# Decoder kernel: where the context of batches 1 to 3 is loaded and split into halves

## What is computed

```python
x = _layernorm(x + _L0_attn_ref(x, ...))             # causal self attention, 32 heads of 16, rope
x = _layernorm(x + _L0_xattn_ref(x, ctx_4096, ...))  # cross attention, 32 heads of 128, 8 key/value heads, 1601 keys
x = _layernorm(x + _L0_ffn_ref(x, ...))              # base matrix plus top 2 of 28 LoRA experts of rank 8
```

## Time and profile before

| | |
|---|---|
| median of 3 runs | 2960.67 us (2955.37 to 2963.62) |
| profiled execution, its own time | 2956.6 us |
| its span, first to last instruction | 2954.8 us |
| mean granted clock of PE | 0.979 of full speed |
| busy: PE, DVE, ACT, POOL | 93%, 71%, 67%, 56% of the span |

### The profile page before, as it was taken

One profiled execution on the slowest core, in us unless ns is written; L12 is line 12 of the kernel. 1 busy time (PEld: TensorE's weight loads), 2 busy tenths in 40 slices (PEclk: granted clock), 3 DMA queues, 4 the chain that ended last, 5 costly groups with the idle time before them and its releaser, 6 DMA issues.

```text
span 2954.8 us, 60508 instructions
## 1 busy us (share of the span) xinstructions
PE 2760.3 (93%) x20272; PEld 2576.1 (87%) x20272; DVE 2100.3 (71%) x4364; ACT 1973.2 (67%) x4392; POOL 1660.6 (56%) x1663
## 2 busy tenths in 40 slices
PE   7899999998899999999899999999988999999996
PEld 6789999998679999999768999999967899999995
DVE  5477777778557878787755877777766587878785
ACT  4476676767457777677655877777756576767673
POOL 4288897947115656565611656555552265656564
PEclk9999999999899999999999999999989999999998
DMA  5446464612311212121331112121232121212112
GB/s 186 139 165 216 160 231 158 211 58 101 119 48 44 94 51 94 51 94 51 122 102 44 63 67 76 69 74 71 78 119 86 42 74 57 89 55 90 55 55 100
DMA packets 97921, 285.10 MB, mean 96 GB/s; under 512 B 9936, under 2 KB 18256, under 8 KB 94416
## 3 DMA queue, kind: packets, MB, share of 16 engines
q1 hardware_dynamic: 97616, 281.24, 27.3%
HBM read 237.16 MB, written 44.04 MB: 95 GB/s over the span
## 4 chain that ended last, share of the span: by engine, by line
PE 67%; issue 11%; POOL 9%; ACT 5%; DVE 5%; DMA 2%; DVEq 0%; ACTq 0%; SPq 0%; POOLq 0%
PE bank L1030 39%; PE dn L1030 14%; PE sp L1030 9%; POOL kept_s L527 4%; ACT ph L714 2%; PE sp L1161 1%; POOL orw L546 1%; PE sp L1169 1%; POOL ol L550 1%; ACT pn L641 1%; PE sp L1101 1%; PE sp L1248 1%; DVE mcol L909 1%; POOL hib L517 1%; ACT sp L719 1%
## 5 line engine op out<-in xcount | busy, mean ns | idle before, releaser
L527 POOL TENSOR_TENSOR kept_s<-kept_s,mrow 128x512 f32<-128x512 f32 (+1 forms) x896 | 1062.3, 1215 | 596.8 <-ACT mrow L704 596.7
L920 DVE TENSOR_TENSOR pl<-sp,ph 128x512 fp32r<-128x512 f32 (+1 forms) x896 | 576.9, 644 | 79.3 <-ACT sp L719 75.8
L714 ACT ACTIVATE ph<-kept_s 128x512 fp32r<-128x512 f32 (+1 forms) x896 | 534.1, 596 | 45.7 <-POOL kept_s L527 42.8
L719 ACT ACTIVATE sp<-kept_s 128x512 f32<-128x512 f32 (+1 forms) x896 | 506.1, 565 | 2.1 <-DVE sua L928 2.1
L1030 PE MATMUL dn<-ph,vh 128*128 128x256 f32 (+1 forms) x1664 | 489.4, 294 | 2.2 <-DVE pl L920 1.7
L1030 PE MATMUL dn<-ph,vl 128*128 128x256 f32 (+1 forms) x1664 | 471.4, 283 | 0.0
L1030 PE MATMUL dn<-pl,vh 128*128 128x256 f32 (+1 forms) x1664 | 470.7, 283 | 0.0
L928 DVE TENSOR_TENSOR sua<-sp,sua 128x512 f32<-128x512 f32 (+1 forms) x640 | 400.2, 625 | 0.0
L696 ACT ACTIVATE kept_s<-bank 128x512 f32<-128x512 f32 x384 | 228.5, 595 | 232.0 <-PE bank L1030 231.4
L696 ACT ACTIVATE kept_s<-sp 128x512 f32<-128x512 f32 x384 | 228.6, 595 | 193.0 <-PE sp L1030 192.6
L1030 PEld LDWEIGHTS dn<-ph,vh 128*128 128x128 f32 (+1 forms) x1664 | 316.5, 190 | 10.3 <-DVE pl L920 3.4
(11 more groups left out here) (149 smaller groups left out, 6967.4 us busy)
## 6 DMA issues: line engine op xcount, KB each, us to landing
wqx<-wq SPq DMA_DIRECT2D x128, 512.0 KB, 3.3
wox<-wo SPq DMA_DIRECT2D x64, 1024.0 KB, 4.8
wk<-wk SPq DMA_DIRECT2D x32, 512.0 KB, 3.3
wvx<-wv SPq DMA_DIRECT2D x16, 1024.0 KB, 5.6
raw<-in_ctx_t SPq DMA_DIRECT2D x48, 200.0 KB, 2.4
wqk<-in_ws SPq DMA_DIRECT2D x17, 513.0 KB, 4.0
raw<-in_wq_in SPq DMA_DIRECT2D x32, 256.0 KB, 3.8
wq<-hib SPq DMA_DIRECT2D x32, 256.0 KB, 2.0
```

Of the source, the lines that this page charges most:

```text
L527: nc.gpsimd.tensor_tensor(kept_s[:, n % 2, i:z, :], kept_s[:, n % 2, i:z, :], mrow[:, n % 2, :].unsqueeze(1).broadcast_to([P, z - i, S]), ...
L714: nc.scalar.activation(ph[:, k % PH, 0:cols], src, ACT.Exp, scale=XSCALE).then_inc(ph_ok, 1)
L719: nc.scalar.activation(pbank[k % 2][:, 0:cols], src, ACT.Exp, scale=XSCALE).then_inc(pr_ok, 1)
L920: nc.vector.tensor_tensor(pl[:, k % PH, 0:cols], src, ph[:, k % PH, 0:cols], ALU.subtract).then_inc(pl_ok, 1)
```

## The change

For batch 0 nothing changes in the self attention. The 16 pieces of batch b+1 (b = 0, 1, 2) are now made in the cross attention of batch b: SP issues the load of piece i at slot 184 + 2i, and ACT's copy and POOL's subtraction of piece i stand at slot 186 + 2i, the last ones at slot 216, each at the end of its engine's slot. A slot g holds POOL's shift of slot g + 4, so the pieces fall behind the shifts s = 1, 3, 5 of head 27, s = 0, 2, 4, 6 of head 28, s = 1, 3, 5 of head 29, s = 0, 2, 4, 6 of head 30 and s = 1, 3 of head 31. ACT's copy waits besides for the last K job, since it overwrites the context. The order of the pieces is now by columns first. The self attention of batches 1 to 3 holds no piece any more.

```diff
--- before.py
+++ after.py
@@ -153,17 +153,30 @@
 HEAD_W = 3
 
 
-def raw_at(b, m, i):
-
-    if b == 0:
-        return m * len(SA_RAW) + i
-    return NM * len(CTX_PIECES) * b + W_N + m * len(CTX_PIECES) + i
+def raw_at(m, i):
+
+    return m * len(SA_RAW) + i
+
+
+CTX_ORDER = [(m, k) for k in range(len(CTX_PIECES)) for m in range(DC)]
+CTX_LOAD, CTX_HIGH = NSL * 26 + 2, NSL * 26 + 4
+
+
+def ctx_piece(g, start):
+
+    i, odd = divmod(g - start, 2)
+    return [i] if not odd and 0 <= i < CTX_N else []
+
+
+def ctx_at(b, i):
+
+    return CTX_N * b + W_N + i
 
 
 def raw_of_weight(k):
 
     if k < NM * SA_W:
-        return raw_at(0, k // SA_W, 2 * (k % SA_W) + 1)
+        return raw_at(k // SA_W, 2 * (k % SA_W) + 1)
     return NM * len(SA_RAW) + k - NM * SA_W
 
 
@@ -414,13 +427,12 @@
                         sp.dma_start(wqk[:, :], ws[m + 1, :, 0:W_QK]).then_inc(wqk_ld, 16)
                         sp.wait_ge(s_vp, at(t, 1, 1))
                         sp.dma_start(wv[:, :], ws[m + 1, :, W_QK:W_QK + D]).then_inc(wv_ld, 16)
-                    for k in range(len(CTX_PIECES)):
-                        load_context(b, m, k, raw_at(b, m, 2 * k if b == 0 else k))
-                        if b == 0:
-                            if k:
-                                store_weight(m * SA_W + k - 1)
-                            if k < SA_W:
-                                load_weight(m * SA_W + k)
+                    for k in range(len(CTX_PIECES) if b == 0 else 0):
+                        load_context(0, m, k, raw_at(m, 2 * k))
+                        if k:
+                            store_weight(m * SA_W + k - 1)
+                        if k < SA_W:
+                            load_weight(m * SA_W + k)
                 if b == 0:
                     load_k(0, 0)
                     load_q(0)
@@ -463,6 +475,9 @@
                             load_k(b * NP + (c + 1) // 2, (c + 1) % 2)
                         elif c + 1 == XKV:
                             load_k(b * NP + NP, 0)
+                    for i in ctx_piece(g, CTX_LOAD):
+                        if b + 1 < nb:
+                            load_context(b + 1, *CTX_ORDER[i], ctx_at(b + 1, i))
                     for j in JOBS[g]:
                         used(j)
                 sp.wait_ge(sc_mm, (b + 1) * NHB * NSL)
@@ -501,10 +516,10 @@
             pool.sem_inc(ot_ok, 1)
             nc.gpsimd.memset(vx[:, :, :, :], 0.0).then_inc(s_vz, 1)
 
-            def ctx_low_part(b, m, k, r):
+            def ctx_low_part(n, m, k, r):
 
                 a, z = CTX_PIECES[k]
-                pool.wait_ge(split_hi, b * CTX_N + m * len(CTX_PIECES) + k + 1)
+                pool.wait_ge(split_hi, n + 1)
                 nc.gpsimd.tensor_tensor(ctxl[:, m, a:z], raw[:, r % 2, 0:z - a], ctxh[:, m, a:z],
                                         ALU.subtract).then_inc(raw_free, 1)
 
@@ -553,10 +568,10 @@
                 pool.wait_ge(x_ld, at(b, 32, 32))
                 for tb in range(TB):
                     nc.gpsimd.tensor_tensor(xres[:, tb, :], xres[:, tb, :], bos[:, :], ALU.add).then_inc(bias_ok, 1)
-                for m in range(NM):
+                for m in range(NM if b == 0 else 0):
                     for k in range(len(CTX_PIECES)):
-                        ctx_low_part(b, m, k, raw_at(b, m, 2 * k if b == 0 else k))
-                        if b == 0 and k < SA_W:
+                        ctx_low_part(m * len(CTX_PIECES) + k, m, k, raw_at(m, 2 * k))
+                        if k < SA_W:
                             split_weight(m * SA_W + k)
                 pool.wait_ge(xt_ps, at(b, 2 * TB, TB))
                 for tb in range(TB):
@@ -568,6 +583,9 @@
                         shift_scores(b, h, s)
                     for h in head_of(g, HEAD_END):
                         finish_head(b, h)
+                    for i in ctx_piece(g, CTX_HIGH):
+                        if b + 1 < nb:
+                            ctx_low_part(CTX_N * (b + 1) + i, *CTX_ORDER[i], ctx_at(b + 1, i))
                     h, s = divmod(g, NSL)
                     if b == 0 and 0 <= h < NHB and s in PIECE_SLOTS:
                         k = NM * SA_W + HEAD_W * h + PIECE_SLOTS.index(s)
@@ -593,8 +611,10 @@
                     nc.scalar.activation(dst[:, :, tb * P:(tb + 1) * P],
                                          mx[:, tb, :].rearrange("p (c n) -> p c n", c=DC), ACT.Copy).then_inc(xt_ok, 1)
 
-            def high_part(hi, src):
-                nc.scalar.activation(hi, src, ACT.Copy).then_inc(split_hi, 1)
+            def ctx_high_part(m, k, r):
+                a, z = CTX_PIECES[k]
+                act.wait_ge(raw_ld[r % 2], 16 * (r // 2 + 1))
+                nc.scalar.activation(ctxh[:, m, a:z], raw[:, r % 2, 0:z - a], ACT.Copy).then_inc(split_hi, 1)
 
             for b in range(nb):
                 act.wait_ge(s_vz, b + 1)
@@ -651,13 +671,8 @@
                         take_qk(m + 1)
                     if i == 7 and m + 1 < NM:
                         take_v(m + 1)
-                    if i in (1, 3, 5, 7) and m < NM:
-
-                        k = i // 2
-                        r = raw_at(b, m, 2 * k if b == 0 else k)
-                        a, z = CTX_PIECES[k]
-                        act.wait_ge(raw_ld[r % 2], 16 * (r // 2 + 1))
-                        high_part(ctxh[:, m, a:z], raw[:, r % 2, 0:z - a])
+                    if b == 0 and i in (1, 3, 5, 7) and m < NM:
+                        ctx_high_part(m, i // 2, raw_at(m, i // 2 * 2))
                 take_heads(NM - 1)
 
                 def job_high(kind, p, i):
@@ -747,6 +762,10 @@
                     for j in JOBS[g]:
                         if j[0] != "O":
                             job_high(*j)
+                    for i in ctx_piece(g, CTX_HIGH):
+                        if b + 1 < nb:
+                            act.wait_ge(job, jobs_to(b, "K", NP - 1, 2 * len(KCH) - 1))
+                            ctx_high_part(*CTX_ORDER[i], ctx_at(b + 1, i))
                 deviation(b, 1)
                 copy_xt(b, 1, xt)
                 act.wait_ge(f_v, at(b, N_FV, 7))
@@ -1128,7 +1147,7 @@
                         last = mm(mx[:, tb, :], ots[:, m, tb * P:(tb + 1) * P], wos[:, m, 0:D], m == 0, m == NM - 1)
                     last.then_inc(s_y, 1)
                 pe.wait_ge(s_res, at(b, 2, 2))
-                pe.wait_ge(raw_free, raw_at(b, NM - 1, 3 if b else len(SA_RAW) - 1) + 1)
+                pe.wait_ge(raw_free, (ctx_at(b, CTX_N - 1) if b else raw_at(NM - 1, len(SA_RAW) - 1)) + 1)
 
                 def scores(h, s):
 
```

## The result

The changed kernel takes 2986.32 us in the median of 4 runs (2980.34 to 2987.49), the kernel before, run beside it, 2962.14 (4 runs, 2955.37 to 2965.03): ratio 1.0081 with an interval of 1.0058 to 1.0103, so 24 us slower (17 to 31). Later runs of the kernel before, in larger numbers, have medians of 2958.13 and 2959.07 us; they did not run beside the changed kernel, but against them it would be 27 to 28 us slower. The profiled execution took 2980.34 us, its span is 2978.5, the mean granted clock 0.974.

A forecast was written before the change was run, and what follows sets the result against it. PE was busy 93% of the span, but POOL's shifts carried the tail's chain of waits. Three tails at +9.5 us (28.5) less 6.7 for the removal gave +21.8, 2978.4, put at 2980 us; range +12 to +32, 2960 to 3000.

The forecast's parts named there:

- The place that receives the work: End of cross attention, batches 0 to 2, heads 27 to 31: pieces and waits add 9.5 us per tail, 28.5 for three.
- A subtraction in slot g waits until ACT has finished its whole slot g: Tail: POOL stands in line behind ACT, next shifts queue behind; waits of 0.9, 0.4 and 0.55 us in head 27.
- All that POOL has to spare: Heads 27 to 31: only POOL's wait for row maxima, 14.5 us, of which 5.2 lie before the first piece.
- the lower bound: Tail: if POOL filled every wait, 15.4 us of pieces less 11.1 of gaps leave about 4 us per tail.
- rival B: Tail: pieces mostly fill POOL's waits, costing 12 us in all, removal brings 6.7: +5, 2966 us; chance 0.18.
- Loads at nothing: Tail: 16 loads, two buffers, each issued four slots ahead of its copy, about 8 us of cover, costed at nothing.
- The removal: Self attention, batches 1 to 3: 1.9 us won per batch, 5.6 for three, plus 1.1 in batch 2: 6.7 us.
- The copies' 0.84 us: Self attention's last group: ACT's copies hold up the next exponential by 0.42 us at two places, 0.84 per batch.
- Batch 2's extra 1.1 us: Batch 2's self attention: first copy waits for its load, 0.63 us idle, then 0.44 until the next exponential.
- No scaling takes over about 0.4 us: Sign in self attention after the change: DVE's scalings, up to 999 ns before, stay at about 0.4 us or less.
- Rival C: Tail: each piece costs POOL's and ACT's time in full, 16.6 us per tail: +43, 3004 us; chance 0.14.
- Rival D: Self attention: PE's idle 7.7 us per batch go nearly all, tail at its lower bound: -11, 2949 us; chance 0.08.

The follow-up runs named there:

- x_low_later: Changed kernel with POOL's subtraction one slot later, ACT's copy left in place: 2964.72 us (10 runs), ratio 1.0022 to the kernel before.
- x_act_later: Changed kernel with POOL's subtraction one slot later and, in batches 1 to 3, cut to 4 columns: 2949.15 us (one run).
- s_act_tiny: Kernel before with ACT's copies of batches 1 to 3 cut to 4 columns: 2959.95 us (one run).
- gaps3: Changed kernel with 13 pieces per batch back in self attention, three at POOL's waits in heads 27 to 29: 2956.24 us, ratio 0.9990 to the kernel before.
- s_pool_tiny: Kernel before with POOL's subtractions of batches 1 to 3 cut to 4 columns: 2955.71 us (one run).

## Why the forecast came out

The forecast was +21.8 us; it came to 24.2 between the medians and 23.7 between the profiled executions, inside the range, and the tail grew by the mechanism that was forecast. That the total agrees within 2 or 3 us is in part luck. The tails cost more than forecast (30.9 us at the same clock, 33.3 in this execution, for 28.5), the self attentions won less (4.7 at the same clock, 3.0 here, for 6.7). Both misses go the same way, 4.8 and 3.7 us in this execution; the 4.6 us by which the first tail started early and the 1.4 behind the tails, which no term of the forecast is about, hide most of them. Step by step:

- **"The place that receives the work" (+9.5 us per tail).** Measured +10.3, +10.3, +12.7. In batch 1 by heads, forecast and measured: 15.8 and 16.15; 15.6 and 15.71; 15.8 and 15.87; 15.6 and 15.20; head 31's part up to the end of its shifts, forecast +2.7, went from 8.92 to 12.18, +3.3. Waits at head 27's pieces: 0.9, 0.4, 0.55 forecast; 0.95, 0.44, 0.71 measured. "A subtraction in slot g waits until ACT has finished its whole slot g" is the step that the runs bear out: with one slot of distance 4.9 of the 10.3 go, with POOL's work gone too 4.3 more.
- **"All that POOL has to spare".** POOL's 15.4 us of work cost only 4.3 once it doesn't wait: the lower bound (pieces less POOL's gaps, about 4) is what x_low_later less x_act_later gives. x_low_later's 2964.72 us lie near rival B's 2966, but not for B's reasons: its three tails cost 5.3 + 5.3 + 6.9 = 17.5 us for B's 12, and all three of its self attentions ran without a fall of the clock.
- **Loads at nothing.** Right: the 16 loads and ACT's copies together cost 1.0 us. No wait for a load of `raw` is among the larger waits of the tail.
- **The removal, 1.9 us per batch and 1.1 more in batch 2 (-6.7 us).** This term was too large. At the same clock it is 1.6, 1.4 and 1.7 us, and the three batches of the profiled execution gave 3.0 us in all. The copies' 0.84 us agree with the measured 0.9 by luck: they were put at two places of the last group, and s_act_tiny wins 0.66 us in the first group and 0.3 behind it. POOL's part was 1.0 forecast and 1.1 alone, but 0.7 on top of the copies, since in the first group either cut alone wins the same 0.7 us. Batch 2's extra 1.1 us behind a load are not there: at clock 1.00 that batch gains 1.4 us in all, where 3.0 were forecast, and less than the other two.
- **"No scaling takes over about 0.4 us".** Right: 350 ns at most. The Trainium skill (SBUF — State Buffer, Who interferes with whom) has VectorE and GpSimd share one port pair, which an instruction that needs it holds to its end. The trace agrees, with a longest scaling of 999 ns beside a subtraction and of 350 without; it does not bear out the reading that all of it lies on the path, by which the gain would have been several times larger: DVE loses 3.1 us to 15.4 us of subtractions, and cutting them wins 1.1. Likewise ACT's 8.8 us of copies come back as 0.9: ACT's waits for DVE's maxima in batch 3 go from 12.6 to 16.1 us when the copies leave.
- **Rival C (full price, 3004) and the clock that may fall earlier.** The clock did fall in head 30: 0.89 in batch 1, where it was 1.00, and 0.78 in batches 0 and 2. It cost nothing visible there: head 30 takes 15.2 us in all three, as POOL is busy 14.6 of it. Nor is it new, as batch 0 of the kernel before has 0.86 there, in the same 12.43 us. It did cost in batch 2's heads 27 and 29, below.
- **Rival D (faster, 2949).** Even with the pieces gone from all three batches the kernel takes 2951.8. The self attention gives back 1.7 us of PE's 7.7 idle ones per batch; the rest, as the rival's own counter-argument had it, belongs to the order scores, maximum, exponential, transposes.

## What to carry to other kernels

Price moved work not by its duration but by where it stands in an in-order engine's program: here the same 16 pieces cost 10.3 us per tail with the subtraction right behind the work of the engine it waits for and 5.3 with it one slot later, and three pieces in slots where POOL waits anyway cost nothing that shows. And before moving work out of a busy stage, leave it out altogether once: 24 us were lost to win what leaving it out entirely bounds at 7.

## What was not expected of the hardware

PE's granted clock falls in one batch and not in another at the same instructions of the same execution, and each such dip has a price that is as large as the gain looked for here. The kernel before, the first 30 us of the self attention of batch 1 and of batch 2 (184 matmuls in each):

```profile
771.60:801.80 30.20, 25.79 (x184) 21.60 (x185) 20.92 (x73) 19.13 (x68) 7.50 (x7) 0.94 0.41 130
1499.75:1528.15 28.40, 24.67 (x184) 20.05 (x185) 19.75 (x73) 19.02 (x68) 7.50 (x7) 1.00 0.42 138
```

In the first of the two the clock stands for 3.4 us at its lower level (1.2 of 2.4 GHz), with PE busy throughout:

```profile
774.90:778.30 3.40, 3.40 (x20) 3.17 (x22) 0.74 (x3) 0.19 (x2) 1.59 (x2) 0.50 0.73 279
```

Work of 1.7 us at the full clock then takes 3.4, which is about what the stretch is longer by. And gaps3, head 27 of batch 1 and of batch 2:

```profile
1388.60:1403.90 15.30, 13.85 (x99) 13.12 (x98) 12.15 (x23) 12.47 (x27) 12.01 (x13) 0.89 0.13 49
2115.40:2129.20 13.80, 12.34 (x99) 11.62 (x98) 12.18 (x23) 12.49 (x27) 12.03 (x13) 1.00 0.16 55
```

1.8 and 1.5 us. Head 27 at a lower clock also appears in s_pool_tiny and s_act_tiny, which have no pieces in the tail, so the pieces are not what brings it. In the changed kernel batch 2's heads 27 and 29 were hit, and there it is 1.2 us each beside batch 1:

```profile
2127.99:2145.34 17.35, 15.31 (x109) 14.57 (x108) 13.77 (x26) 14.30 (x31) 13.89 (x14) 0.90 0.20 68
...
2161.04:2178.14 17.10, 15.45 (x102) 13.87 (x101) 12.76 (x25) 13.21 (x28) 13.70 (x15) 0.90 0.53 172
```

That is the 2.4 us by which its third tail passed the other two, though POOL is as full there. x_low_later and x_act_later ran their self attention of batch 3 in 75.6 us, without a dip, for 77.17 after. What decides whether a given stretch dips was not tried, and whether x_act_later's 2949.15 us is more than an execution with few dips stays open with one run.
